# Loading raw expert weights in halves, each half on its own semaphores

## The reference, cut to what matters

```python
def _L0_ffn_ref(x, gate_w, ln_gamma, ln_beta, fc1s, b1s, fc2s, b2s):
    xf = x.reshape(-1, d)                        # 8224 rows, d = 256
    k = int(bs * CAPACITY) // n                  # n = 8 experts, k = 1028
    scores = (jnp.tanh(xf @ gate_w.T) + 1.0) * 0.5
    vals, idx = jax.lax.top_k(scores.T, k)
    y = _layernorm(xf[flat_idx].reshape(k, n, d), ln_gamma, ln_beta)
    h = jnp.einsum('knd,nfd->knf', y, fc1s) + b1s    # 1024 hidden
    h = jax.nn.gelu(h, approximate=True)
    o = (jnp.einsum('knf,ndf->knd', h, fc2s) + b2s) * kept_w[:, :, None]
    out = xf.at[flat_idx].add(o.reshape(k * n, d))
```

## Time and profile before

| what | value |
|---|---|
| median of 3 runs | 878.05 us (875.82 to 880.17) |
| profiled execution | 877.11 us |
| its span in the profile | 875.2 us |
| mean granted clock of TensorE | 0.919 of full speed |
| busy share of PE, DVE, ACT, POOL | 85%, 66%, 52%, 53% |
| DMA | 64.32 MB, mean 73 GB/s |

### The profile page before, as it was taken

The page is one execution under the profiler, slowest core; times in us unless marked ns, Lnnn a source line. Parts: engine busy times, 40 slices in busy tenths (PEclk is TensorE's granted clock), DMA queues, the critical chain, the costliest instruction groups (busy, mean ns, idle before and its releaser), DMA issues.

```text
span 875.2 us, 15546 instructions
## 1 busy us (share of the span) xinstructions
PE 743.0 (85%) x4349; PEld 627.9 (72%) x4349; DVE 580.8 (66%) x1951; ACT 452.6 (52%) x998; POOL 463.5 (53%) x744
## 2 busy tenths in 40 slices
PE   6977999999999972333799897998979989989994
PEld 3644666766676652222698897998979979889994
DVE  3835888888888866988776574574656836544341
ACT  1003677777777763000553765545646655366552
POOL 0127667776777743203336556565475664654723
PEclk9988999999999995555899999998999999989997
DMA  9400121122112226201123233334243342323312
GB/s 347 184 3 1 49 73 54 66 72 72 59 61 72 73 73 108 102 1 44 61 38 95 72 52 87 86 51 128 38 98 79 49 133 43 96 69 51 50 19 31
DMA packets 45448, 64.32 MB, mean 73 GB/s; under 512 B 13840, under 2 KB 40528, under 8 KB 42704
## 3 DMA queue, kind: packets, MB, share of 16 engines
q1 hardware_dynamic: 32400, 46.54, 15.9%
q0 software_dynamic: 12800, 17.12, 12.0%
q10 hardware_dynamic: 192, 0.00, 0.0%
HBM read 38.12 MB, written 25.53 MB: 73 GB/s over the span
## 4 chain that ended last, share of the span: by engine, by line
PE 32%; DVE 8%; issue 8%; POOL 7%; DMA 4%; ACT 3%; POOLq 1%; ACTq 0%; DVEq 0%; SPq 0%
PE bank L885 15%; PE bank L899 12%; DMA raw<-in_fc1T 3%; DVE ge L1242 2%; POOL w2l L494 2%; POOL yg L509 2%; POOL out L531 2%; DVE Tc L1258 1%; PE bank L874 1%; ACT bank L668 1%; PE bank L922 1%; PE bank L864 1%; PE bank L911 1%; DMA yg<-rows,idx 1%; ACT hh L671 1%
## 5 line engine op out<-in xcount | busy, mean ns | idle before, releaser
L1365 DVE TENSOR_TENSOR hl<-bank,hh 128x384 fp32r<-128x384 f32 (+1 forms) x192 | 97.5, 513 | 167.7 <-ACT hh L671 165.4
L531 POOL DMA_INDIRECT out<-ob,sidx x72 | 113.9, 1582 | 165.4 <-ACT ob L684 153.8
L668 ACT ACTIVATE bank<-bank,b1s 128x384 f32<-128x384 f32 (+1 forms) x192 | 99.5, 518 | 134.4 <-PE bank L885 133.9
L885 PE MATMUL bank<-yh,w1h 128*128 128x384 f32 (+1 forms) x384 | 137.8, 359 | 27.4 <-DVE hl L1365 26.1
L885 PE MATMUL bank<-yh,w1l 128*128 128x384 f32 (+1 forms) x384 | 127.5, 332 | 0.0
L885 PE MATMUL bank<-yl,w1h 128*128 128x384 f32 (+1 forms) x384 | 127.4, 332 | 0.0
L899 PE MATMUL bank<-w2l,hh 128*128 128x256 f32 x384 | 108.0, 281 | 0.0
L899 PE MATMUL bank<-w2h,hh 128*128 128x256 f32 x384 | 108.0, 281 | 0.0
L899 PE MATMUL bank<-w2h,hl 128*128 128x256 f32 x384 | 107.9, 281 | 0.0
L509 POOL DMA_INDIRECT yg<-rows,idx x72 | 72.4, 1006 | 62.9 <-issue 57.8
L885 PEld LDWEIGHTS bank<-yh,w1h 128*128 128x128 f32 x384 | 77.3, 201 | 32.7 <-DVE hl L1365 28.7
(11 more groups left out here) (223 smaller groups left out, 1760.9 us busy)
## 6 DMA issues: line engine op xcount, KB each, us to landing
BIG<-in_x SPq DMA_DIRECT2D x4, 2048.0 KB, 18.9
out<-Bs SPq DMA_DIRECT2D x32, 256.0 KB, 2.2
rows<-Yp SPq DMA_DIRECT2D x32, 256.0 KB, 2.4
raw<-in_fc1T SPq DMA_DIRECT2D x8, 1024.0 KB, 4.8
raw<-in_fc2T SPq DMA_DIRECT2D x8, 1024.0 KB, 4.8
yg<-rows,idx POOLq DMA_INDIRECT x72, 2.9
out<-ob,sidx POOLq DMA_INDIRECT x72, 3.8
gwb<-in_gate_w SPq DMA_DIRECT2D x1, 1024.0 KB, 12.4
```

The source lines that it names most:

```text
L531: g.indirect_dma_start(out=out_rows, out_offset=tok(ap=sidx[job.eh][0:m, t:t + 1], axis=0), in_=ob[t % 3][0:m, :], in_offset=None, compute ...
L668: A.activation(h[:, 0:cur.w], h[:, 0:cur.w], ACT.Gelu_apprx_tanh, bias=b1s[:, bass.ds(cur.e, 1), f]).then_inc(s["hact"], 1)
L885: last = T.matmul(Lb[ring(cur, f)][:, 0:cur.w], w1s[cur.eh][i][:, d, f * P:(f + 1) * P], yT[cur.p][k][:, d, 0:cur.w], start=(n == 0), stop ...
L1365: v.tensor_tensor(hT[cur.p][1][:, f, 0:cur.w], Lb[ring(cur, f)][:, 0:cur.w], hT[cur.p][0][:, f, 0:cur.w], ALU.subtract).then_inc(s["hlo"], 1)
```

## The change

`raw` is treated as two halves of 128 x 1024. Each has its own semaphores, `wld0` and `wld1` for landed, `wlo0` and `wlo1` for subtracted. SP issues two transfers of 512 KB per weight; the transfer of a half waits for the subtraction of that half alone. ACT's `high` waits for its own half, POOL's `low` signals after each half, and PE waits for both counters where it waited for one. Arithmetic, tiles and the order of work on each engine stay.

```diff
--- before.py
+++ after.py
@@ -228,7 +228,7 @@
             xc xc_l z_done zw inv q h0 st0_b st0 var pow nrm st_set hcE et et_ev er er_ev eg_ev sm nmax pexp pt pt_ev av u h1 rv
             st1_b st1 tug teg base yp tab base_st0 base_st1 yp_st0 yp_st1
             gt_c gt_t gt_v vt_st vsp_t vsp thr tc cn t_tried t_range t_next tk_c tk_mm oh_begun oh_first
-            ohd smm smc ixc ixd wld bld0 bld1 whi wlo hhi hlo yhi yr gat00 gat01 gat02 gat10 gat11 gat12 yt_t yt hmm hact om oadd omul omt oev obk scat0 scat1 scat2 idc""".split()
+            ohd smm smc ixc ixd wld0 wld1 bld0 bld1 whi wlo0 wlo1 hhi hlo yhi yr gat00 gat01 gat02 gat10 gat11 gat12 yt_t yt hmm hact om oadd omul omt oev obk scat0 scat1 scat2 idc""".split()
         s = {n: sem(n) for n in names}
 
         def after(eng, name, count):
@@ -389,13 +389,13 @@
 
             def weights(el, eh, layer):
                 q, e = el * 2 + eh, el + 4 * eh
-                after(sp, "wlo", q * 2 + layer)
-                if layer == 0:
-                    sp.dma_start(raw[:, :], fc1T[bass.ds(e, 1), :, :].rearrange("e p c -> p (e c)"))\
-                        .then_inc(s["wld"], 16)
-                else:
-                    sp.dma_start(raw[:, :], fc2T[bass.ds(e, 1), :, :].rearrange("e p c -> p (e c)"))\
-                        .then_inc(s["wld"], 16)
+
+                for half in range(2):
+                    part = slice(half * NF, (half + 1) * NF)
+                    after(sp, f"wlo{half}", q * 2 + layer)
+                    sp.dma_start(raw[:, part], (fc1T, fc2T)[layer][bass.ds(e, 1), :, part].rearrange("e p c -> p (e c)"))\
+                        .then_inc(s[f"wld{half}"], 16)
+                if layer:
                     after(sp, "oadd", (q - 1) * 6)
                     sp.dma_start(b2b[eh][:, :], b2[bass.ds(e, 1), :].partition_broadcast(P).rearrange("p e d -> p (e d)"))\
                         .then_inc(s[f"bld{eh}"], 16)
@@ -492,8 +492,7 @@
                 hi, lo = (w1s, w2s)[layer][eh]
                 po.wait_ge(s["whi"], (q * 2 + layer) * 2 + half + 1)
                 rest = g.tensor_tensor(flat(lo, half), raw[:, half * NF:(half + 1) * NF], flat(hi, half), ALU.subtract)
-                if half:
-                    rest.then_inc(s["wlo"], 1)
+                rest.then_inc(s[f"wlo{half}"], 1)
 
             for layer in range(2):
                 for half in range(2):
@@ -643,7 +642,7 @@
             def high(eh, q, layer, half):
 
                 hi = (w1s, w2s)[layer][eh][0]
-                act.wait_ge(s["wld"], (q * 2 + layer + 1) * 16)
+                act.wait_ge(s[f"wld{half}"], (q * 2 + layer + 1) * 16)
                 A.activation(flat(hi, half), raw[:, half * NF:(half + 1) * NF], ACT.Copy).then_inc(s["whi"], 1)
 
             def high_rows(job):
@@ -925,14 +924,16 @@
             def emit(prev, cur, nxt, tiles):
                 if cur:
                     if cur.c == 0:
-                        pe.wait_ge(s["wlo"], cur.q * 2 + 1)
+                        for half in range(2):
+                            pe.wait_ge(s[f"wlo{half}"], cur.q * 2 + 1)
                     pe.wait_ge(s["yt"], cur.j + 1)
                 for f in SLICES:
                     if cur:
                         first(cur, f)
                     if prev:
                         if prev.c == 0 and f == 0:
-                            pe.wait_ge(s["wlo"], prev.q * 2 + 2)
+                            for half in range(2):
+                                pe.wait_ge(s[f"wlo{half}"], prev.q * 2 + 2)
                         for u, n in second(prev, f):
                             (token_term if prev.c < 2 else tail_term)(prev, u, n)
                         if prev.c == 2 and f == BACK_AT:
```

## The result

The changed kernel takes **848.7 us** (median of 4 runs, 847.95 to 849.17) against 876.93 before in the same comparison; the ratio is 0.9667, 95% interval 0.9649 to 0.9685. Forecast were 848, range 842 to 862. So the medians differ by 28.2 us, where the prediction took 30 off; the profiled execution took 848.66 us, 28.45 less than that of before.

The account below looks back on a forecast made before the run. PE was taken to stall behind ACT's early wait for fc1 weights, then run partly at the lower clock. Six times 5.0 us, 30, off the profiled 877.11 gave 847.1; from the median 878.05, 848; range 842 to 862.

Parts of the forecast that it names:

- The wait and its path: In experts 1 to 6, ACT waits for fc1's load, delaying gelu, DVE's hl and PE; 34.3 us at most to gain.
- place: Stretch from the last L911 group to the next job's first L899, six per run, 11.82 us each before.
- A half lands in 3.1 us: SP's 512 KB weight load was taken to land in 3.1 us, against 4.8 for a whole 1 MB.
- the 4 us that the prediction had named as a sign of being wrong: The prediction called itself wrong if a half load takes over 4 us.
- The line through 256 KB and 1 MB: Landing time of a half load, interpolated between 2.2 us for 256 KB and 4.8 for 1 MB: 3.1 us.
- 5.0 us at each place, 30 in all: From the last L911 group to L899: 6.8 us against 11.82, 5.0 less at each of six.
- What is late next: DVE's yl, behind the second half, was to be late by 0.7 us over the undisturbed 6.10.
- fc2, the longer queues, the gathers: Split fc2 loads, 16 more SP transfers and gathers sharing the engines: nothing; PE's extra waits bounded by 2.9 us.
- The search: Threshold search before the experts, where GpSimd's subtractions lengthen DVE's TL by 5.2 us: change taken as 0, between -1.8 and +4.2.
- rival 4: Half 1 lands late, sharing DMA engines with GpSimd's gathers: 889 us at a 10 us landing; chance 0.03.
- rival 3: Something in SP's order holds half 0 until half 1 may go: 2.7 us saved each, 862; chance 0.03.
- Rival 4's slope: Each us of later landing of half 1 costs 6 us of time over the six places; chance 0.03.

Follow-up runs that it names:

- the first experiment: The changed kernel, but both fc1 halves leave only when the second half of the buffer is free: 867.95 us, ratio 0.9876 to the kernel before.

## Why the prediction was right, point by point

*The wait and its path.* Right. Half 0 leaves after the first subtraction, ACT's waits were put at some 4 us per place and 24 us in all, and measured 3.9 and 23.2. The undoing of the early issue alone took away 19 us of the 28 (18 by the ratios).

*A half lands in 3.1 us.* A little low: 3.2 to 3.8 us, in one case (half 0 at the fourth place) 4.1. That one passes the 4 us that the prediction had named as a sign of being wrong; the fourth place was the shortest all the same, 6.23 us. The line through 256 KB and 1 MB was the right choice between its ends of 2.2 and 4.8. The Trainium skill's fit for one DMA (DMA: Bandwidth & Descriptors, Anatomy of one DMA) gives 3.2 us; eleven of the twelve lie within 0.6 of it, and the twelfth is 0.9 above. The Trainium skill's rule of 1 MiB or more per DMA (same page, Rules for kernel authors) did not decide here: the DMA engines' share is far from full, 0.37 to 0.47 in the places shown, and what counted was when ACT could begin. Whole loads asked for later gave more all the same, so the rule cost nothing to keep. The other rule that the prediction cites is about halves of the partitions; the halves here are column halves, with all 128 partitions in each.

*5.0 us at each place, 30 in all.* Measured 29.1, since the places took 6.97 us on average instead of 6.8. What is late next was named rightly, yl behind the second half, and PE's 0.34 us before slice 0 of the next job shows it; the wait for oT before it, 0.4 us at most places, was in the working as "waits for DVE" at next to no cost of its own (some 0.15 us).

*fc2, the longer queues, the gathers.* Taken at nothing; the run with fc2's split undone shows it for fc2, and PE's wait for the gathers' rows from 455 to 790 us is 0.6 us.

*The search.* Taken at 0 between -1.8 and +4.2. TL's lengthening fell from 5.2 to 4.39 us, and the stage before the experts from 401.01 to 400.06 us. The pairs did not come apart (4.66 and 4.65 us for the two), because the second half is there and copied by ACT before the first one's subtraction ends:

```profile
347.11 1.07 DVE L1248 TENSOR_SCALAR TL<-Tc 128x2 f32<-128x2 f32 x1
...
349.47 1.02 DVE L1248 TENSOR_SCALAR TL<-Tc 128x2 f32<-128x2 f32 x1
...
355.01 1.91 DVE L1248 TENSOR_SCALAR TL<-Tc 128x2 f32<-128x2 f32 x1
...
358.20 1.02 DVE L1248 TENSOR_SCALAR TL<-Tc 128x2 f32<-128x2 f32 x1
```

*What was missed.* The clock in rival 4 and in rival 3. Rival 3 was priced at 2.7 us per place, 862; built as the first experiment it took 868. It was also worked from the sixth place's 12.30 us where the average is 11.82, which makes it 2.2 per place, or 9.6 us for a place. Measured were 10.42 on average: 9.94 and 10.19 at full clock in the first two, 10.01 to 11.65 in the four with a lower clock. Rival 4's slope of 1 us per us of landing and place was 5.7 us for 4.5. The forecast does not depend on either, for in it PE never stands long. And 1.7 us of the gain at the places went where the prediction had not looked, most of it at the loop's turn.

*What was luck.* The mechanism was right, but the nearness of the total, 28.3 us of span for 30, is helped by terms that offset each other: 0.9 too much at the places and 1.7 lost elsewhere, against 0.95 gained before the experts, where the prediction had taken nothing.

*What the prediction didn't ask*: whether the load had to come sooner at all. Its first paragraph says that nobody needs these weights for three jobs; the cheaper remedy, a later place in ACT's queue, follows from that sentence, and beats the change by 3 to 4 us.

## What to carry to other kernels

When an engine waits long for a transfer, ask two things before making the transfer faster: who needs the data, and what stands behind the waiting instruction in its queue. If the need lies far off, move the instruction down its queue or give the transfer its own buffer; making it quicker removes only part of the wait. Price each stall of TensorE with what the clock does afterwards, and look for the small stalls that the large one covers (here PE's waits for oT and yl), for they take their share when it goes.

## What the runs showed of the hardware

A stand of PE of 3.64 us is followed by matmuls at the lower level (0.69 us for the first, against 0.44 behind a wait at full clock; the places' granted clock was 0.72 to 0.85, a mix of 2.4 and 1.2 GHz), while stands of up to 1.4 us in the changed kernel leave it at 1.00. Between the two the length of the stand does not settle it. With the fc1 halves together, a stand of 2.10 us in the first place went with clock 1.00 and one of 2.09 us in the fifth with 0.83; the first and the fourth place, at 1.00 and 0.71, lie 1.7 us apart. With every half fetched twice, a stand of 3.34 us in the first place went with 0.76 and one of 3.58 us in the fifth with 1.00.

GpSimd's subtraction, which reads two tiles in SBUF, held up more of DVE's instructions than the small TL: the scans, and in the run with copies behind slices 2 and 5 one TH, which took 2.33 us instead of 0.16. Moving it from the search into the scans cost 6.7 us at one wait where it had cost 4.4 in TL. The Trainium skill states it (SBUF — State Buffer, SBUF: two separate sides): of a GpSimd instruction that reads SBUF and a VectorE instruction with two inputs in SBUF, or in a mode that uses both its ports, the one that started first keeps the shared ports for its whole length, and the other stands. The trace agrees for TL, which ends with GpSimd's instruction; that the scans are slowed by the same thing is argued from their overlap and was not tried by itself. The cause of DVE's stand at the loop's turn is open: it was 1.6 us with whole loads and with the fc1 halves together, and 2.8 to 3.3 us in the changed kernel and in the runs with only fc2's halves together and with the later first subtractions.
